# First-pass scores in chunks of 384 columns by a table, and GpSimd masking two rows of probabilities per visit

## The reference

```
q, k, v = xh @ Wq + bq, xh @ Wk + bk, xh @ Wv + bv      # 8 heads of 16 features
content   = einsum('bqhd,bkhd->bhqk', q + u_bias, k)
pos_score = rel_shift(einsum('bqhd,khd->bhqk', q + v_bias, p))
attn      = softmax((content + pos_score) / sqrt(e), axis=-1)
ctx       = einsum('bhqk,bkhd->bqhd', attn, v)
```

## Time and profile before

| what | value |
|---|---|
| median of three runs | 1685.92 us |
| profiled execution | 1683.95 us |
| its span, first to last instruction | 1682.2 us |
| share of the span busy: PE, VectorE, ScalarE, GpSimd | 92%, 83%, 66%, 66% |
| mean granted TensorE clock | 0.952 |
| DMA, mean | 119 GB/s |

### The profile page before, as it was taken

The page is one execution under the profiler, slowest core; times in us unless marked ns, Lnnn a source line. Parts: engine busy times, 40 slices in busy tenths (PEclk is TensorE's granted clock), DMA queues, the critical chain, the costliest instruction groups (busy, mean ns, idle before and its releaser), DMA issues. The chain is left out here.

```text
span 1682.2 us, 51020 instructions
## 1 busy us (share of the span) xinstructions
PE 1549.5 (92%) x12534; PEld 1207.6 (72%) x12535; DVE 1402.2 (83%) x5272; ACT 1113.2 (66%) x2303; POOL 1106.0 (66%) x2090
## 2 busy tenths in 40 slices
PE   3789999999999999999999999999951799999997
PEld 1567777677676767777767776767731799999997
DVE  4669899989989987998998998899854588888886
ACT  2157776776777776677777777767730577777775
POOL 5257767767766775776677677677663276666666
PEclk8689999999999998999999999999975899999999
DMA  5746535535644553464364355346454243443433
GB/s 136 198 116 177 145 94 156 163 93 130 183 111 122 163 155 85 104 198 108 104 185 136 96 160 164 97 122 189 113 147 127 43 59 52 56 57 51 57 53 48
DMA packets 134404, 199.99 MB, mean 119 GB/s; under 512 B 20936, under 2 KB 95576, under 8 KB 134192
## 3 DMA queue, kind: packets, MB, share of 16 engines
q1 hardware_dynamic: 108336, 177.21, 39.1%
q0 software_dynamic: 25856, 20.27, 7.8%
HBM read 108.24 MB, written 75.33 MB: 109 GB/s over the span
## 5 line engine op out<-in xcount | busy, mean ns | idle before, releaser
L1083 DVE CUSTOM_DVE_ANT_0 junk<-pA,lmask 128x512 bf16<-128x512 f32 x1056 | 686.8, 682 | 63.1 <-PE pA L670 44.1
L985 ACT ACTIVATE prob<-pB 128x512 f32<-128x512 f32 x384 | 229.9, 599 | 204.5 <-PE pB L689 115.8
L1576 POOL DMA_INDIRECT out<-yb,dst x144 | 230.9, 1604 | 134.9 <-ACT yb L1650 82.5
L691 PE MATMUL pB<-QL,K 97*128 97x512 f32 (+3 forms) x768 | 285.7, 372 | 1.4 <-ACT upper_diag L985 1.4
L668 PE MATMUL pA<-K,QL 96*128 96x512 f32 (+3 forms) x792 | 281.8, 357 | 5.0 <-DMA K<-split_operands 3.2
L689 PE MATMUL pB<-QU,K 97*128 97x512 f32 (+3 forms) x640 | 267.1, 417 | 0.3
L670 PE MATMUL pA<-K,QU 96*128 96x512 f32 (+3 forms) x660 | 233.1, 354 | 4.5 <-DVE acc L1083 3.2
L987 ACT ACTIVATE prob<-pB 128x512 f32<-128x512 f32 x384 | 227.8, 593 | 12.7 <-PE pB L691 4.5
L707 PE MATMUL pC<-prob,vext 128*17 128x256 f32 x3088 | 217.4, 384 | 0.1
L575 POOL TENSOR_TENSOR prob<-prob,upper_diag 128x128 f32<-128x128 f32 x384 | 180.2, 469 | 32.0
L689 PEld LDWEIGHTS pB<-QU,K 97*128 97x128 f32 x640 | 121.9, 190 | 99.4 <-issue 59.3
(11 more groups left out here) (305 smaller groups left out, 3656.5 us busy)
## 6 DMA issues: line engine op xcount, KB each, us to landing
QL<-split_operands SPq DMA_DIRECT2D x67, 256.0 KB, 3.7
QU<-split_operands SPq DMA_DIRECT2D x67, 256.0 KB, 4.1
K<-split_operands SPq DMA_DIRECT2D x67, 256.0 KB, 4.4
xg<-routed_rows SPq DMA_DIRECT2D x76, 132.0 KB
split_operands<-c_h SPq DMA_DIRECT2D x36, 256.0 KB, 6.1
split_operands<-c_l SPq DMA_DIRECT2D x36, 256.0 KB, 6.4
QL<-split_operands SPq DMA_DIRECT2D x67, 128.0 KB, 3.6
QU<-split_operands SPq DMA_DIRECT2D x67, 128.0 KB, 4.1
```

The lines of the kernel that those rows point to most:

```text
L691: mm = pe.matmul(pB[:, q0 + up:q0 + HALF], K[0:r, s, k], QL[0:r, s, q0 + up:q0 + HALF], start=True, stop=True)
L985: act.activation(p[:, 0:HALF], pB[:, 0:HALF], ACT.Exp, scale=SCALE).then_inc(p_exp, 1)
L1083: v.tensor_tensor_reduce(out, src[:, :], lmask[:, at:at + HALF], 1.0, -3.0e38, ALU.add, ALU.max, acc[:, s, qb, n % 2:n % 2 + 1]).then_inc( ...
L1576: po.indirect_dma_start(dram["out"], bass.IndirectOffsetOnAxis(dst[k][:, a:a + 1], 0), yb[k][:, a, :], None, compute_op=ALU.add).then_inc( ...
```

## The change

Three things are changed.

1. The first pass goes in 24 chunks of 384 columns for each head (three for each query block) instead of 16 pieces of 512 and 2 of 4 x 128. The lower form takes the chunk's first columns, the upper form starts over at the diagonal block, so the key range of a query block is 1024 + 128 = 1152 columns = 3 x 384. One mask `smask` replaces `lmask` and `umask`. A table `SHARE` says how many chunks each (head, unit) issues, 1 to 4: the first before second pass half 1, two behind it, a fourth behind the context pair. Still three PSUM buffers.
2. GpSimd masks rows kb and kb + 1 together in even units (2, 4, 6, 8): memsets, one affine_select and one add over 2 x 128 columns. Both rows are released together.
3. The six low parts of `c`, `k`, `gl` and the `dsup` of each head move from VectorE to GpSimd (`SPLIT_AT`, `DSUP_AT`), and positions, scatters and a residual half move mostly to odd units.

```diff
-S1U = NB * HPB + HPB
+CHUNK = 3 * P
+SPANS = (S + P) // CHUNK
+S1U = NB * SPANS
...
-        prob = [keep["b2"]] + [sb(f"prob{i}", [P, S]) for i in range(1, RING)]
+        ring = [keep["b2"], sb("prob23", [P, 2, S])]
+        prob = [ring[i // 2][:, i % 2, :] for i in range(RING)]
...
-        LOW_AT = {(1, 2): 0, (2, 3): 1, (2, 7): 2, (3, 2): 3, (3, 6): 4, (4, 1): 5, (4, 3): 6, (4, 4): 7}
-        POSITIONS_AT = ((1, 1), (1, 4), (1, 8), (2, 1), (2, 4), (2, 6), (5, 4), (5, 6))
+        LOW_AT = {(3, 6): 4, (4, 4): 7}
+        SPLIT_AT = {(0, 3): 0, (1, 8): 1, (2, 8): 2, (3, 3): 3, (3, 7): 5, (4, 2): 6}
+        DSUP_AT = 3
+        POSITIONS_AT = ((1, 1), (1, 3), (1, 7), (2, 1), (2, 3), (2, 5), (5, 5), (5, 7))
...
-        ORDER = (0, 1, 2, 3, 4, 5, 6, 7, 16, 8, 9, 10, 17, 11, 12, 13, 14, 15)
+        SHARE = ((3, 2, 3, 3, 3, 3, 2, 3, 2), (3, 2, 3, 3, 3, 3, 2, 3, 2), (2, 2, 3, 2, 3, 3, 3, 2, 4), (1, 3, 2, 2, 4, 2, 3, 3, 4),
+                 (3, 4, 2, 2, 2, 3, 2, 2, 4), (3, 2, 1, 3, 4, 3, 2, 2, 4), (3, 4, 3, 3, 3, 3, 2, 1, 2), (3, 2, 2, 2, 4, 3, 2, 2, 4))
...
         def piece(n):
-            qb, k0 = n // HPB, (n % HPB) * HALF
-            return qb, k0, min(max(P * (qb + 1) - k0, 0), HALF)
+            qb, c = divmod(n, SPANS)
+            return qb, c, min(max(P * (qb + 1) - CHUNK * c, 0), CHUNK)
...
+            def low(nb, n):
...
+                po.wait_ge(hi_done, have)
+                po.tensor_tensor(parts[name][1][:, cut], src, parts[name][0][:, cut].bitcast(F32), ALU.subtract).then_inc(low_done, 1)
+
+            def super_difference(b, h):
...
+                po.wait_ge(mx_done, have)
+                po.tensor_tensor(dsup[:, s, :], acc[:, s, :, 3], mneg[:, s, :].bitcast(F32), ALU.add).then_inc(dsup_done, 1)
...
-                        else:
-                            kb = u - 1
-                            if kb > 0:
-                                po.memset(prob[kb % RING][0:1, P * kb - 1:P * kb], 0.0)
-                            p = prob[kb % RING][:, P * kb:P * kb + P]
+                        elif u % 2 == 0:
+                            kb = u - 2
+                            both_rows = ring[kb // 2 % 2][:, :, :].rearrange("p a s -> p (a s)")
+                            for k in (kb, kb + 1)[kb == 0:]:
+                                po.memset(prob[k % RING][0:1, P * k - 1:P * k], 0.0)
+                            p = both_rows.rearrange("p (n q) -> p n q", q=P)[:, kb:kb + NB + 2:NB + 1, :]
                             po.affine_select(out=p, in_=p, compare_op=ALU.is_ge, fill=0.0, base=0,
-                                             pattern=[[1, P]], channel_multiplier=-1).then_inc(lower_masked, 1)
+                                             pattern=[[0, 2], [1, P]], channel_multiplier=-1).then_inc(lower_masked, 1)
...
-                            po.tensor_tensor(p, p, upper_diag[h % 2][:, P * kb:P * kb + P], ALU.add).then_inc(p_mask, 1)
+                            po.tensor_tensor(p, p, upper_diag[h % 2][:, P * kb:P * kb + 2 * P].rearrange("p (n q) -> p n q", q=P), ALU.add).then_inc(p_mask, 2)
+                        if u == DSUP_AT:
+                            super_difference(b, h + 1)
+                        if (h, u) in SPLIT_AT:
+                            low(b + 1, SPLIT_AT[h, u])
...
-                        second_pass(b, h, u, 0)
-                        first_pass(b, h + AHEAD, 2 * u)
+                        chunks = share(h, u)
+                        second_pass(b, h, u, 0)
+                        for n in chunks[:1]:
+                            first_pass(b, h + AHEAD, n)
                         second_pass(b, h, u, 1)
-                        first_pass(b, h + AHEAD, 2 * u + 1)
+                        for n in chunks[1:S1_BUFS]:
+                            first_pass(b, h + AHEAD, n)
                         if u in PAIRS_AT:
                             back, kb = PAIRS_AT[u]
                             context(b, h + back, kb)
                             context(b, h + back, kb + 1)
+                        for n in chunks[S1_BUFS:]:
+                            first_pass(b, h + AHEAD, n)
```

More of the change, by code:

```diff
@@ L315, in _ @@
                 sp.wait_ge(hi_done, READY[name])
[L316 removed]
+                if name == "gu":
+                    sp.wait_ge(gu_low, GU_N)
+                else:
+                    sp.wait_ge(low_done, LOWS[name])
                 store_side(name, 0)
@@ L1067, in low @@
                 v.wait_ge(hi_done, nb * HI_N + n + 1)
-                v.tensor_tensor(parts[name][1][:, cut], src, parts[name][0][:, cut].bitcast(F32), ALU.subtract).then_inc(low_done, 1)
+                v.tensor_tensor(parts[name][1][:, cut], src, parts[name][0][:, cut].bitcast(F32), ALU.subtract).then_inc(gu_low if name == "gu" else low_done, 1)
             def super_out(src, done):
@@ L1097, in maxima @@
                 v.tensor_reduce(mneg[:, s, :], acc[:, s, :, :], AX.X, ALU.max, negate=True).then_inc(mx_done, 1)
-                v.wait_ge(mx_done, b * H + h + 1)
-                v.tensor_tensor(dsup[:, s, :], acc[:, s, :, 3], mneg[:, s, :].bitcast(F32), ALU.add).then_inc(dsup_done, 1)
             def row_out(h, src, done):
@@ L1298, in _ @@
                 stats(1, t)
-            for n in range(4, LOW_N):
+            for n in range(4, HI_N):
                 low(0, n)
@@ L1322, in _ @@
                                 small_piece(b, name)
-                        first_pass(b, h + AHEAD, 2 * u + 1)
+                        for n in chunks[1:]:
+                            first_pass(b, h + AHEAD, n)
                         if h == 0 and u in NORMALIZE_AT:
```

94 lines of the change are left out of this document (46 added, 48 removed).

## The result

The changed kernel takes **1711.82 us** (median of four runs, 1711.49 to 1716.51) where the kernel before took 1688.13 in four runs beside it: ratio 1.0144, 95% interval 1.012 to 1.0168. So it is slower by 1.4%. Forecast was 1660 (1648 to 1680), faster. The span is 1710.0 us, the mean granted clock 0.944 instead of 0.952. Start, tail and expert phase are alike. The loss is in the batches: in the trace, the first second-pass matmul of one batch follows that of the batch before it by 146.2 us (144.6 in two of the batches) where it followed by 141.5 (147.7 in one); the first batch takes 152.7 where it took 149.4.

A forecast was written before the change was run, and what follows sets the result against it. TensorE was taken as the bound, covered almost without a gap, with VectorE second at 91% busy. Terms 19 + 8 + 2 - 3 - 1 = 25 us off 1684 gave 1659, stated as 1660, range 1648 to 1680.

The forecast's parts named there:

- Part 1: First pass on TensorE: cutting it into 384-column chunks saves 0.30 us a head, 19 us in all.
- The doubtful pitch: Start-to-start time of a lone 384-column chunk on TensorE: taken as 0.17 us; 0.23 would lose 50 us.
- the wait for `hr`: TensorE's 7.3 us wait before transposing `hr`: expected under 1 us; 8 of 10.1 us won together with `rows_r`.
- the 19 us: Gain on TensorE from the first pass's new cut, 0.30 us a head over 64 heads.
- Part 2: Where the table puts chunks among context and other units: counted as nothing, bounds plus 3 to minus 4 us.
- Part 3: VectorE relieved of low parts and `dsup`: 8 us from two TensorE waits, 2 from `acc`, minus 3 for buffers.
- that for `rows_r`: TensorE's 2.8 us wait before transposing `rows_r`: expected to shrink; 8 of 10.1 us won together with `hr`.
- the charge of 3 us: Cost of three PSUM buffers holding 1.44 us of VectorE's reductions instead of 1.83; bounds 0 and 45 us.
- the 25 that I had named as the sign of being wrong: First-pass weight loads on TensorE: waits for `acc` grown past 25 us would show the prediction wrong.
- the 14.9 that I used: First-pass weight loads' waits for `acc` before the change, taken as 14.9 us, of which 2 would be won.
- The rival "VectorE becomes the bound": VectorE's reductions and small work stop TensorE 0.7 us a head, 45 us more, 1704 us; slower cases' chance 0.10.
- Part 4: GpSimd's two-row mask and moved work: its load stays, contexts wait little more for it; charged 1 us.

The follow-up runs named there:

- experiment 9: Changed kernel with head 6's row (3,2,3,3,3,3,2,3,2) and added VectorE waits, which came out as 8 more instructions a batch: 1680.54 us, ratio 0.9954.
- Experiments 3 and 4: Changed kernel, first with head 6's row (3,2,3,3,3,3,2,3,2): 1683.79 us; second with its original row plus eight filler matmuls of 384 columns a batch: 1696.37 us.
- experiment 13: Changed kernel with another table, new rows for heads 0 to 7 and few four-chunk units, two-row mask kept: 1681.76 us, ratio 0.9969.
- experiment 16: Changed kernel with another table for all heads, mask row by row and five low parts back on VectorE: 1667.98 us, ratio 0.9868.
- experiment 15: Changed kernel with head 6's row (3,2,3,3,3,3,2,3,2), mask row by row and five low parts back on VectorE: 1668.18 us, ratio 0.9874.
- experiment 14: Kernel before the change with the first pass in two of its three PSUM buffers: 1738.41 us, ratio 1.0271.
- experiment 11: Changed kernel with head 6's row (3,2,3,3,3,3,2,3,2) and the six low parts back on VectorE: 1680.34 us, ratio 0.9959.
- experiment 10: Changed kernel with head 6's row (3,2,3,3,3,3,2,3,2) and 24 one-element VectorE memsets more in a batch: 1722.52 us, ratio 1.0198.
- experiment 1: Kernel before with only the cut into 384-column chunks and its table; mask row by row, low parts and dsup on VectorE: 1743.46 us, ratio 1.0331.

## Why the prediction was wrong

Most of the gains were there, the losses weren't in the sum. From the changed kernel down, each step one run: row of head 6, 28 us by the medians and 30 by the ratios (1.0144 to 0.9964); mask of two rows, 10 and 6 (to 0.9927; 7 against the run of experiment 9 on the same chip); five low parts, 5 and 9 (to 0.9874). Between chips the split is no finer than that. Together it is 44 to 46 of the 50 to 52 us by which the forecast missed.

**Part 1, the cut on TensorE: the pitch right, its worth not shown by itself.** The doubtful pitch is 0.17 in the row above and 0.18 in the median over six batches. It is longer only behind a matmul of 128 columns (0.23, as argued) and ahead of a context pair (0.27). The version with the repairs has batches of 138.9 us where the clock holds, the kernel before had 141.5 and the forecast 138.3. That its ratio is 0.9874, some 21 us, and the sum was 25, fits. But 0.9 of its 2.6 us a batch stand in unit (5,3), where the wait for `hr` is gone, and no run has the cut without the stop of VectorE or another part of the change, so how much of the 19 us came isn't known.

**Part 2, the table at zero, plus 3 to minus 4: wrong, and the largest error.** I counted how many chunks stand in context units and never set each row of the table beside VectorE's small work. The fourth chunk in unit (6,1) stands ahead of `rq`; the logits wait, TensorE grows thin, and the clock falls in every batch. The slow clock was in no term and in no rival (the sum took the 1.00 of the earlier trace rows for every batch), though the kernel before shows one such stretch in its loop, at the same place of a batch. Experiments 3 and 4 show both halves of this price.

**Part 3, VectorE: the wait for `hr` right, that for `rows_r` wrong, the charge of 3 us too small.** The wait for `hr` is gone (7.3 to 0). That for `rows_r` rose from 2.8 to 4.5. The table that I called thin there makes it: with the row (3, 2, 3, 2, ...) for head 3 it is 0.4 (experiment 13) and 0.0 (experiment 16), though the first instruction still takes 0.42 and 0.79 us, while with (1, 3, 2, 2, ...) it stays at 3.8 when that instruction takes 0.17 (experiment 15). The waits for `acc` grew to 85.0 us, past the 25 that I had named as the sign of being wrong (a sign set too close, since all rows of before made 23.1 and not the 14.9 that I used). Even with the repairs they are 61.6, yet the time falls: some of what TensorE saves it waits away. That the smaller buffer makes these waits is likely, by experiment 14, but not shown. The rival "VectorE becomes the bound" named the right waits and a time near to what came, 1704, but for a reason that doesn't hold: VectorE didn't have too much work (experiment 11), it was held up at single places. That the number was near is luck.

**Part 4, GpSimd at 1 us: wrong.** The durations were right, and so was that contexts don't wait for it. What I left out is what GpSimd's instructions do to VectorE's. The row for it stood in the earlier trace rows: 1.09 us for 8 elements. I used it as the price of small work. It ran from 432.19, beside GpSimd's select of `upper_diag`, which took 1.10 us from 432.16; with no long instruction of GpSimd beside it, it takes 0.17. The prediction quoted the rule of the Trainium skill ("GPSIMD Engine Reference", Key points: contention with VectorE's instructions of two SBUF inputs or in a 2-port mode) and drew from it that fewer would meet when the low parts move. The runs agree with the rule (the instruction of 8 elements has one SBUF input, so by the rule it would have to be in such a mode, which no run here shows) and not with that inference. A long instruction on GpSimd holds up VectorE's element-wise instructions between SBUF tensors that it meets, not just its own counterpart, and a low part lasts 1.29 us on GpSimd where VectorE needs 0.68. Not all is held up: `BATCH_NORM_STATS2` on 128x128 in SBUF takes 0.26 us with and without GpSimd beside it, and the reductions keep their 0.48.

Not in any part: moving the low parts had a use that I didn't see. The cut needs a wait for each of its 24 chunks where there were 18 pieces, two instructions each and 96 more in a batch, and with all its old work VectorE's loop goes from 894 to 990 and stands for 4 us in every batch. That stop is worth some 39 us in experiment 10, and it is in the time of experiment 1.

What stays open: where between 979 and 990 that stop begins and why, the curve of the buffer's price, what the cut is worth alone, and why in some versions the clock falls in every second batch and in others in one or none.

## What to carry to other kernels

A duration in a trace holds what ran beside it: before you price an instruction of VectorE, look at what GpSimd was doing, and at the shortest row of the same kind. Moving work from VectorE to GpSimd is paid by the element-wise instructions of VectorE on SBUF tensors that it then meets, so keep GpSimd's instructions short and away from those that TensorE waits for. Compare batches one by one, with the granted clock of each: a stretch of 3.4 us at half clock made 1.5 us here that looked like the price of a placement. And read a table of placements row by row against the small work of the engine that is waited for; two chunks of one row were worth 28 us here.

## What the hardware showed that was not expected

- An 8-element instruction on VectorE took 1.19 us beside a GpSimd subtraction of 1.29 us and 0.17 with none of that length beside it; an addition of 128 x 64 took 0.84 beside an add of 0.73, and 0.30 otherwise. Reductions with an operand in PSUM kept their pitch of 0.48, and `BATCH_NORM_STATS2` from SBUF its 0.26.
- 24 memsets of one element in a batch cost 39 us, through a stop of VectorE of 3.4 to 4.6 us at the start of each batch, directly behind the loop's branch and with nothing waited for, and half clock behind it. At 979 instructions in the loop it isn't there, at 990 it is.
- TensorE fell to half its clock after two waits of 0.25 us and eight matmuls of 16 columns, while its row for that stretch reads 6.95 us busy out of 7.50. Eight more matmuls of 384 columns in each batch there made the kernel 15 us faster.
